# Fifteen inverse square roots of a two-layer block moved to VectorE: a guess from the bits and three Newton steps

## The reference

```python
x = x + tanh(g_xattn[0]) * wkv(w, u, layernorm(x), ctx)          # a scan over time with running maximum
x = x + tanh(g_ffn[0])   * quantised_ffn(layernorm(x), w_gate, w_up, w_down)
x = x + tanh(g_xattn[1]) * attention(layernorm(x), ctx, Wq, Wk, Wv)   # 32 heads of 8, q and k rms-normed
x = x + tanh(g_ffn[1])   * experts(layernorm(x), ...)            # 64 experts, top 8, and a shared one

layernorm(x) = (x - mean) / sqrt(var + 1e-5)                      # over 256 values
rmsnorm(t)   = t * rsqrt(mean(t * t) + 1e-6)                      # over the 8 values of a head
```

## Time and profile before

| | |
|---|---|
| median of 3 runs | 531.2 us (530.32 to 532.62) |
| profiled execution | 528.41 us, of which the span is 526.6 us |
| TensorE busy | 406.7 us (77% of the span) |
| VectorE busy | 347.1 us (66%), 722 instructions |
| ScalarE busy | 284.0 us (54%), 431 instructions |
| GpSimd busy | 49.2 us (9%) |
| mean granted TensorE clock | 0.939 of full speed |

### The profile page before, as it was taken

The page is one execution under the profiler, slowest core; times in us unless marked ns, Lnnn a source line. Parts: engine busy times, 40 slices in busy tenths (PEclk is TensorE's granted clock), DMA queues, the critical chain, the costliest instruction groups (busy, mean ns, idle before and its releaser), DMA issues.

```text
span 526.6 us, 7351 instructions
## 1 busy us (share of the span) xinstructions
PE 406.7 (77%) x2602; PEld 195.1 (37%) x2606; DVE 347.1 (66%) x722; ACT 284.0 (54%) x431; POOL 49.2 (9%) x37
## 2 busy tenths in 40 slices
PE   1101534729668778977799999999999999999994
PEld 1001222315344333433344444444444444444442
DVE  5899599894874664765497567656566565554553
ACT  2855482757785989887655255343343343432321
POOL 0725732001100111000000000000000000000000
PEclk9999955887995999998799999999999999999998
DMA  8400000000001000004530335523333433412211
GB/s 306 165 1 0 1 0 1 1 0 1 0 2 60 1 1 2 2 1 131 151 109 22 111 103 171 183 89 136 128 103 121 139 104 108 131 60 69 71 62 40
DMA packets 24576, 38.01 MB, mean 72 GB/s; under 512 B 4826, under 2 KB 11354, under 8 KB 24028
## 3 DMA queue, kind: packets, MB, share of 16 engines
q1 hardware_dynamic: 24540, 37.54, 22.2%
HBM read 36.21 MB, written 1.31 MB: 71 GB/s over the span
## 4 chain that ended last, share of the span: by engine, by line
PE 58%; DVE 18%; ACT 11%; issue 7%; DMA 2%; POOL 1%; SPq 1%; ACTq 0%; DVEq 0%
PE ps L1140 33%; PE ps L1413 15%; ACT regA L646 3%; DVE regA L801 1%; DVE xn L769 1%; PE ps L1162 1%; PE ps L1197 1%; PE ps L1297 1%; DVE regA L790 1%; PE ps L1340 1%; DMA regA<-in_dp_dram 1%; PE ps L1327 1%; PE ps L1132 1%; ACT regB L551 1%; DMA x<-in_x_dram 1%
## 5 line engine op out<-in xcount | busy, mean ns | idle before, releaser
L1140 PE MATMUL ps<-hH,regB 128*128 128x512 f16 x512 | 164.0, 382 | 0.0
L698 ACT ACTIVATE regA<-ps 128x512 f32<-128x512 f32 x65 | 38.8, 597 | 146.8 <-PE ps L1140 144.9
L1098 DVE TENSOR_TENSOR regA<-ps,regA 128x512 f32<-128x512 f32 x65 | 45.0, 692 | 99.8 <-ACT regA L698 99.8
L1140 PE MATMUL ps<-hL,regB 128*128 128x512 f16 x256 | 97.8, 382 | 0.0
L1413 PE MATMUL ps<-regA,regB 128*128 128x512 f16 x384 | 93.4, 379 | 1.3 <-DVE regA L1103 1.3
L1140 PEld LDWEIGHTS ps<-hH,regB 128*128 128x128 f16 x512 | 50.4, 98 | 61.7 <-issue 2.9
L646 ACT ACTIVATE regA<-ps 128x1024 f32<-128x1024 f32 x64 | 62.0, 1025 | 10.9 <-PE ps L1327 10.0
L1413 PEld LDWEIGHTS ps<-regA,regB 128*128 128x128 f16 x384 | 37.3, 98 | 47.3 <-DVE regA L1103 2.3
L1103 DVE TENSOR_TENSOR regA<-regA 128x512 f16<-128x512 f32 x65 | 44.3, 682 | 0.7 <-ACT regA L690 0.7
L1108 DVE TENSOR_TENSOR regA<-regA 128x512 f32<-128x512 f32 x65 | 44.5, 685 | 0.2 <-DMA regA<-routing_dram 0.2
L690 ACT CAST regA<-regA 128x512 f16<-128x512 f32 x65 | 39.7, 610 | 1.5 <-DVE regA L1108 1.5
(11 more groups left out here) (171 smaller groups left out, 521.8 us busy)
## 6 DMA issues: line engine op xcount, KB each, us to landing
regA<-routing_dram SPq DMA_DIRECT2D x130, 128.0 KB, 3.0
regA<-in_gu_dram SPq DMA_DIRECT2D x32, 256.0 KB, 2.6
regA<-in_dp_dram SPq DMA_DIRECT2D x32, 128.0 KB, 2.7
regA<-in_ffn_dram SPq DMA_DIRECT2D x2, 1024.0 KB, 8.3
x<-in_x_dram SPq DMA_DIRECT2D x2, 512.0 KB, 3.9
ctxT<-in_ctxT_dram SPq DMA_DIRECT2D x1, 1024.0 KB, 8.2
regB<-in_ffn_dram SPq DMA_DIRECT2D x1, 1024.0 KB, 12.3
out_dram<-x SPq DMA_DIRECT2D x2, 512.0 KB, 3.3
```

What stands on the lines that cost most here:

```text
L698: nc.scalar.activation(sgm[:, c % 2, :], bank(GATE_BANK[c % 2]), ACT.Silu, scale=UNSCALE).then_inc(esilu_done, 1)
L1098: V.tensor_tensor(sgm[:, c % 2, :], bank(GATE_BANK[c % 2] + 1), sgm[:, c % 2, :], ALU.mult).then_inc(et_done, 1)
L1140: mm = T.matmul(out_ap, w(k), a(k), start=(n == 0), stop=(n == 3 * DK - 1))
```

## The change

Ln and Exp on ScalarE, their two semaphores and the tiles `lnv` and `root` are gone. `inverse_root` on VectorE does the whole root in twelve instructions, each waiting for the one before: the variance plus epsilon (with the gain squared divided out), a shift of its bits to the right by one, that number taken from a constant, which gives a first guess, and three Newton steps of three instructions. It stands where `root_end` stood, for rows run 0 and 1 as well, so nothing of a root is issued ahead any more.

In ScalarE's code fifteen rounds of two activations go, and with them the two pairs of table loads at t = 0 and t = 4 of the feed-forward loop and the pair round norm 8. The load at t = 6 moves behind the loop, ahead of the first two query splits. The pair round the routing's exponentials stays.

```diff
@@ scalar: the feed-forward loop
                 if t == 1:
                     tokens_to_integers(1)
                     turned_integers(1, 0)
-                elif t == TT - 2:
-                    nc.scalar.preload_act_table_set(EXP_LN)
-                elif t == TT - 1:
-                    first_root(2 * HEADS)
                 ffn_turned(t)
-                if t == 0:
-                    nc.scalar.preload_act_table_set(EXP_LN)
-                    first_root(HT * HEADS)
-                    first_root(HT)
-                    nc.scalar.preload_act_table(ACT.Silu)
-                elif t == 4:
-                    nc.scalar.preload_act_table_set(EXP_LN)
-                    first_root(HT)
-                    nc.scalar.preload_act_table(ACT.Silu)
                 if t + 2 < TT:
                     ffn_silu(t + 2)
...
                     project(8, bank(0))
                     project(9, bank(1))
+            nc.scalar.preload_act_table_set(EXP_LN)
             split(8)
             split(9)
@@ scalar: the experts
-                    if name in ("norm", "weigh"):
+                    if name == "weigh":
                         nc.scalar.preload_act_table_set(EXP_LN)
                     beside(name, i, 2)
-                    if name in ("norm", "weigh"):
+                    if name == "weigh":
                         nc.scalar.preload_act_table(ACT.Silu)
@@ vector
-            def root_begin(src, n, mul, eps):
...
-            def root_end(n, gain):
...
+            def inverse_root(src, n, mul, eps, gain):
+                v, r, t = ve[:, 0:n], rstd[:, 0:n], newt[:, 0:n]
+                link(V.tensor_scalar(v, src, mul / gain ** 2, eps / gain ** 2, ALU.mult, ALU.add))
+                link(V.tensor_scalar(t.bitcast(I32), v.bitcast(I32), 1, None, ALU.logical_shift_right))
+                link(V.tensor_scalar(r.bitcast(I32), t.bitcast(I32), -1, ROOT_GUESS, ALU.mult, ALU.add))
+                for i in range(3):
+                    link(V.scalar_tensor_tensor(t, r, -0.5, v, ALU.mult, ALU.mult))
+                    link(V.tensor_tensor(t, t, r, ALU.mult))
+                    link(V.scalar_tensor_tensor(r, t, 1.5, r, ALU.add, ALU.mult))
...
             for n in range(HT):
                 project(n)
-            rows_begin(0)
             norm(2, 1.0)
             token_scales(0)
-            rows_end(0)
+            rows(0)
             sums(2)
```

More of the change, by code:

```diff
@@ L44 @@
 MAGIC = 12582912.0
+ROOT_GUESS = 1597463007
 NEG = -1e38
@@ L75, in bass_flamingo @@
         mv = sb("mv", [P, TT, 2])
-        ve = sb("ve", [P, 2, P])
-        lnv = sb("lnv", [P, P])
-        root = sb("root", [P, 2, P])
+        ve = sb("ve", [P, P])
         newt = sb("newt", [P, P])
@@ L439, in settle @@
                 act.wait_ge(a_ord, done[0])
[L441 to L451, removed]
             def abs_sum(m):
@@ L657, in beside @@
                     project(i, bank(6))
-                elif name == "rows":
-                    first_root((ROW_RUNS[i][1] - ROW_RUNS[i][0]) * HEADS)
                 elif name == "split":
                     split(i)
-                elif name == "norm":
-                    first_root(NORM_TILES[i][1] - NORM_TILES[i][0])
                 elif name == "weights":
@@ L731, in _ @@
             V = nc.vector
-            begun, ended = [0], [0]
-            def root_begin(src, n, mul, eps):
-                e = begun[0]
-                begun[0] += 1
-                V.tensor_scalar(ve[:, e % 2, 0:n], src, mul, eps, ALU.mult, ALU.add).then_inc(var_ready, 1)
-            def root_end(n, gain):
-                e = ended[0]
-                ended[0] += 1
-                v, r = ve[:, e % 2, 0:n], root[:, e % 2, 0:n]
-                dve.wait_ge(var_ready, e + 1)
-                dve.wait_ge(root_ready, e + 1)
-                link(V.tensor_tensor(newt[:, 0:n], v, r, ALU.mult))
-                link(V.tensor_tensor(newt[:, 0:n], newt[:, 0:n], r, ALU.mult))
-                link(V.tensor_scalar(newt[:, 0:n], newt[:, 0:n], -0.5 * gain, 1.5 * gain, ALU.mult, ALU.add))
-                link(V.tensor_tensor(rstd[:, 0:n], newt[:, 0:n], r, ALU.mult))
+            def inverse_root(src, n, mul, eps, gain):
[7 more added lines that the diff above has]
+                    link(V.scalar_tensor_tensor(r, t, 1.5, r, ALU.add, ALU.mult))
             def stats(q):
@@ L759, in stats @@
                 settle()
-                root_begin(mv[:, a:b, 1], b - a, 1.0, LN_EPS)
             def norm(q, gain):
                 a, b = NORM_TILES[q]
-                root_end(b - a, gain)
+                inverse_root(mv[:, a:b, 1], b - a, 1.0, LN_EPS, gain)
                 if q in FORMER:
@@ L836, in project, with rows @@
                                 AX.X, ALU.add).then_inc(sq_read, 1)
[L838 removed]
+            def rows(r):
                 a, b = ROW_RUNS[r]
                 dve.wait_ge(sq_read, b)
[L841 to L846 removed]
+                inverse_root(ss[:, (a % HT) * HEADS:(a % HT + b - a) * HEADS], (b - a) * HEADS, 1.0 / HD, RMS_EPS, 1.0)
                 dve.wait_ge(proj_read, b)
@@ L980, in _ @@
                 if t == 1:
-                    rows_end(1)
+                    rows(1)
                     norm(3, 1.0)
@@ L997, in _ @@
             project(9)
-            rows_begin(2)
-            rows_end(2)
+            rows(2)
             split(8)
@@ L1052, in beside @@
                 elif name == "rows":
-                    rows_begin(i)
-                    rows_end(i)
+                    rows(i)
                 elif name == "turn_rows":
```

13 lines of the change are left out of this document (1 added, 12 removed).

## The result

The changed kernel took 548.94 us (median of 4 runs, 548.23 to 550.75), the kernel before 531.91 us beside it (530.32 to 535.21): a ratio of 1.036, with a 95% interval of 1.0318 to 1.0403. The prediction was 547.3 us in a range of 540 to 556. The profiled execution of the changed kernel took 550.75 us, of which the span is 549.0, at a mean granted clock of 0.927.

A forecast was written before the change was run, and what follows sets the result against it. No engine bounds the whole; each root was read by itself. Terms 3.0 + 1.1 + 4.0 + 1.2 + 5.3 + 1.5 = 16.1 us on 528.4 gave 544.5, plus 2.8 to the median 547.3 us, range 540 to 556.

The forecast's parts named there:

- The price of a step: Each chained VectorE root step: 0.195 us at 128x4, 0.31 at 128x128, 0.25 at 128x64, unseen forms alike.
- The rival with dearer steps: All fourteen roots: unseen instruction forms cost more, a root 0.5 us dearer, giving 553 us; no chance of its own.
- Start: Norms 0 and 1, where VectorE works without a pause: two longer roots cost +3.0 us.
- Norm 2 and run 0: Longer roots less VectorE's saved wait for ScalarE, part of the delay being GpSimd's: +1.1 us, bounds 0.9 and 1.3.
- Norm 3 and run 1: Behind the first residual, ScalarE already waits for VectorE, so the longer roots count in full: +4.0 us.
- Norm 4, the load, run 2: End of the feed-forward part: longer norm and uncovered table load of 1.28 us make the query cast late, +1.2 us.
- The attention: Norms 5, 6, 7 and rows runs 3, 4, 5: longer roots delay ScalarE and TensorE, +5.3 us.
- rival (a): Attention: TensorE's clock falls once more, half speed for 6 us adding 4 us, giving 551; chance 0.27.
- Norm 8: In the experts: eight more steps open a gap in TensorE, which bounds everything after, +1.5 us.
- From the profile to the median: Whole kernel: the runs' median, 531.2 us, lies 2.8 above the profiled execution's 528.4, so 2.8 is added.
- Rival (b): Attention and the place before: part is absorbed as scores and probabilities run ahead, giving 544 or 538 us; chance 0.18.
- Rival (c): Feed-forward and attention: ScalarE's queue is what is late, so the change is not slower, 523 us; chance 0.04.

The follow-up runs named there:

- scalar_back: Changed kernel with ScalarE's fifteen Ln/Exp rounds and all table loads back in their old places, results unused; 549.28 us, ratio 1.0353 to the kernel before.
- two_newton: Changed kernel with two Newton steps instead of three in every root, less exact, for timing only; 540.08 us, ratio 1.0197 to the kernel before.
- filled2: Changed kernel with 50 unread filler products in TensorE's attention waits, in a PSUM bank free at that moment; 547.18 us, ratio 1.0305 to the kernel before.
- early_merged: Kernel before with norm 2's and run 0's ScalarE rounds ahead of the exponentials and one root for norms 0 and 1; 528.71 us, ratio 0.9971.
- routes_after: Changed kernel with SyncE's first four pairs of routing-row loads ahead of the attention's last weight load; 548.13 us, ratio 1.0333 to the kernel before.
- routes_norm8: Changed kernel with the first routing rows loaded earlier and norm 8's root alone the old way; 545.31 us, ratio 1.0281 to the kernel before.
- routes_early: Kernel before with norm 2's and run 0's rounds earlier, norms 0 and 1 sharing one root, and routing rows loaded earlier; 526.42 us, ratio 0.9919.
- attn_new: Kernel before with only the attention's six roots on VectorE by twelve steps; 538.91 us, ratio 1.0147 to the kernel before.

## Why the prediction was right, and where it was not

The direction and the mechanism stand: at nearly every root VectorE's chain is what the next engine waits for, eight more steps lengthen it, and what ScalarE is relieved of lay in its waits. scalar_back and two_newton show these two halves apart. One of the signs that I had named for being wrong did come, though: a low clock in the attention's middle. Point by point:

- **The price of a step** held: 0.20 us at 128x4, 0.31 at 128x128, 0.25 at 128x64. The two forms without a row cost what the others do. The rival with dearer steps (553) falls.
- **Start**, +3.0: 3.1 and 3.2.
- **Norm 2 and run 0**, +1.1: 0.8 and 0.1, and 1.1 and 1.7 in two more. Right in sign and size. GpSimd's share in it was not tried.
- **Norm 3 and run 1**, +4.0: 4.5 and 6.0, and twice 4.0. ScalarE's wait was 11.31 us where I said near 12. The surplus, 0.75 and 1.9 us, is there before run 1, at the first residual. Its cause is open: the mean clock in 110 to 160 (0.84 and 0.80, before 0.89) does not account for it, as filled2 had 0.83 and cost 4.0.
- **Norm 4, the load, run 2**, +1.2: 2.3, 0.8, 1.0 and 1.4. The size was right for a wrong reason. I had the load uncovered at 1.28 us and the twelve steps beside it; they are as long as each other, and taking the load out alone is worth 0.2.
- **The attention**, +5.3: 8.4 to 9.6 in the traces, 7 to 8 in the times. This is the mis-sized term. Its waits are 5.5 us, near what I had summed. The rest is rival (a), the clock, which I had at 4 us and a chance of 0.27. Its 4 us agree with the 3 to 4 that the traces leave by luck: I had 6 us at 1.2 GHz, each costing two thirds of a microsecond, and it was 10 to 14 us, costing a quarter to a third each. I had also held the wrong thing against it, that one gap of 2.0 us had not brought the clock down: in early_merged the same gap did. The change made four gaps (2.53, 1.79, 1.9 and 2.2 us within 25 us), and the fillers that shortened them kept the clock up but for one fall. That more gaps make a fall likelier is argued from this; what sets the falls off is not shown. I said TensorE would wait 4 us at one place. It waits at two, since norm 5's transposes stand ahead of the product.
- **Norm 8**, +1.5: TensorE waited 0.87 and 0.30 us. The mechanism and the price were right (1.68 us in routes_after against routes_norm8), but the step "the engine that bounds everything after" overlooked a late transfer in front of it, which had 0.24 us to spare before and now was waited for. "To the experts" came to 2.0 and 2.9 us, mostly by way of that row.
- **From the profile to the median**, +2.8: here two errors met. The sum was 5 to 6 us short of the two traces, and the profiled execution of before was further below its median (3.5) than that of after from its own. The median is hit within 1.6 us partly by this luck. What the executions of before spend in the runs that are 3 us longer, no profile of it shows. Its one profile has no fall in the attention, and early_merged's, with the same roots there, has two and spends 1.4 us more; falls of that kind in its other executions would bring the 8.4 to 9.6 of the traces to the 7 to 8 of the times. That is argued, not shown.
- **Rival (b)**, an absorbed part, is not seen at any root but norm 8, and there a late transfer hid the steps, not work that ran ahead. **Rival (c)**, ScalarE's queue as the one that is late, is refuted by scalar_back: with ScalarE's queue as long as before the time is 0.5 us more, where that rival asks for some 10.

## What to carry to other kernels

An operation moved from a second engine into a chain of small dependent steps is priced by steps times the start-to-start time of one, at each place where another engine is queued behind it; what the relieved engine saves counts only where it was late. Where the cover of a cost is part of the same change, as with the load and the twelve steps, undo one alone before giving it a price. And an edit that gives nothing where it should may be behind a late transfer: move that issue earlier first, and try the edit again.

## What the hardware showed

- A dependent VectorE step of 2 to 4 columns takes 0.20 us from start to start and is busy for 0.16 to 0.17, in every form tried, int32 shift and multiply among them. 45 such steps gave 0.17 to 0.19 us each at the end of the kernel. The Trainium skill (VectorE: DVE Perf Modes, the section on the TRN2 errata) has 58 cycles as the fixed part in its table, about 65 ns for four columns, and that is the figure that the prediction set against the trace. The same section says below the table that this row comes out too low and gives (N + 151) / 0.96 ns for an fp32 `tensor_tensor`, from 512 and 2048 columns. For four columns that makes an estimate of 161 ns, and the trace bears it out with 0.16 us busy; the 0.03 to 0.04 us from the end of a step to the start of the next come on top.
- A table load on ScalarE took 1.28 us, and the next activation began 0.02 us behind it, also with another activation ahead (110.21 and 111.51 above). The Trainium skill (ScalarE: Activation LUTs, "What ACT_TABLE_LOAD costs") adds a drain of 1380 ns. These rows leave no room for it.
- TensorE's granted clock fell from 2.4 to 1.2 GHz four times in the attention of the changed kernel, which has four gaps of 1.8 to 2.5 us there. But a gap does not settle it: the same wait ahead of query product 12 was followed by the full clock in the kernel before (2.01 us) and in routes_early (2.03), and by 1.2 GHz in early_merged (2.04). Some 10 to 14 us at 1.2 GHz went with 3 to 4 us that no waiting row shows (an estimate, from 8.4 and 9.6 less the 5.5 of the waits in attn_new): products start 0.21 us apart instead of 0.11.
- A low clock elsewhere can be free. The profiled execution of routes_early had a mean of 0.52 from 24 to 60 us, and at 526.04 us was faster than any profile of another kernel here: TensorE had 7 us of work in those 36.
